# A fused transformer kernel on one core: in the quantised FFN, gated values are quantised two passes behind, the rounding unit comes from a square on ScalarE, and GpSimd has no pass

## The chip, the cores and the metric

The kernel runs on one core of one Trainium2 chip. The metric is the device time of one execution in microseconds (us). Beside it stands one profiled execution, with the start and the duration of every instruction on TensorE (PE; PEld for its weight loads), VectorE (DVE), ScalarE (ACT), GpSimd (POOL) and the DMA queue of SyncE (SP).

## What is computed

Six blocks in a row act on x of 16 x 256 tokens by 128 features: a quantised FFN, an attention of low rank, the quantised FFN again, a mixture of experts, a windowed attention, and the experts again. Only the quantised FFN is touched:

```
def fp4_quant_dequant(x):                       # blocks of 16 along the last axis
    scale = max(max(abs(block)) / 6, 1e-12)
    xn = block / scale
    idx = searchsorted(_MID, abs(xn))           # _MID = .25 .75 1.25 1.75 2.5 3.5 5
    return _GRID[idx] * sign(xn) * scale        # _GRID = 0 .5 1 1.5 2 3 4 6
def fp4_linear(x, w): return quant_dequant(x) @ quant_dequant(w).T
h = silu(fp4_linear(x, w_gate)) * fp4_linear(x, w_up)   # 128 -> 352
x = x + 0.5 * fp4_linear(h, w_down)                     # on layernorm(x)
```

## The kernel before

Everything stays in SBUF as tiles of 128 tokens. An FFN phase (class `Ffn`, run 0 and run 1) makes 16 passes, each over two tiles (256 tokens), and all phases are written engine by engine with semaphores; each engine runs its own list in order. One pass z on each engine:

- ScalarE: normalises the two tiles of pass z+1 into `xh` (L328, one operation a tile), copies the transposed x out of PSUM to `xqT` (L343), copies the transposed h of pass z-2 to `hqT` (L348, L349), and applies silu to the gate product, `sg` (L354).
- VectorE: product of `sg` and the up result in PSUM into the h columns of `xh` (L248, pass z-2), then `quantise` over all 960 columns at once, 256 of x of pass z and 704 of h of pass z-2: block maxima (L101), scale (L104), its inverse (L105, L106), xn = value times inverse (L107), then three operations that make a rounding constant from xn and add it: exponent mask (L114), lower bound (L115), sum (L116). Then the residual add of pass z-3 (L265) and two bn_stats for the next layer norm (L184).
- GpSimd: `dequantise`: subtracts the rounding constant (L140) and multiplies by the scale into `xhq` (L142). L104 of the next pass waits for L142, since it overwrites the scale.
- TensorE: waits for `xhq`; transposes x (L293, 2 matmuls) and h (L299, 6), then gate and up (L307, 8 instructions in the trace), then down (L316, 12).

`rounds` orders the passes: 0 to 2 unrolled, a loop, and three at the end (18 in all). The weights are quantised once at the start by the same two functions, and other phases use `xh`, `xhq`, `q_xn`, `q_mg` for other things. The phases are separated: each engine drains and all wait for each other.

Of the kernel before, what the change touches and what calls it, by code (L numbers as in the profile page):

```python
# [12 lines left out]
F32 = mybir.dt.float32  # L13
# [16 lines left out]
EXPO, HALF = 0x7F800000, 0x00400000  # L30
MAGIC = 1.5 * 2.0 ** 22
NUDGE = 1.0 - 2.0 ** -22

H, DH = 16, 8
SL = 64
# [16 lines left out]
def ds(start, n):  # L52
    return slice(start, start + n) if isinstance(start, int) else bass.ds(start, n)
# [139 lines left out]
class Ffn:  # L193
# [2 lines left out]

    N = NT // 2
    XC, HC_, ALL = (0, 2 * D), (2 * D, 2 * D + 2 * I0), (0, 2 * D + 2 * I0)  # L200

    def __init__(self, k, run):

        self.k, self.run = k, run
        self.x0 = run * self.N
        self.q0 = run * (self.N + 2)
        self.s_xn = k.sem("ffn_xn")
        self.s_xn_read = k.sem("ffn_xn_read")
        self.s_rounded = k.sem("ffn_rounded")
        self.s_minus = k.sem("ffn_minus")  # L210
        self.s_scaled = k.sem("ffn_scaled")
# [10 lines left out]
    def rounds(self, eng, fn, ch=None, per=0):  # L222

        n = self.N
        fn(0, True, False, False)
        fn(1, True, False, False)
        fn(2, True, True, False)
        with eng.Fori(3, n - 1) as z:
            if ch:
                ch.enter(z - 3, per)  # L230
            fn(z, True, True, True)
            if ch:
                ch.leave(n - 4)
        fn(n - 1, True, True, True)
        fn(n, False, True, True)
        fn(n + 1, False, True, True)

    def cols(self, x, h):
        return self.ALL if x and h else self.XC if x else self.HC_

    def vector(self, eng, ch):
        k, v = self.k, self.k.nc.vector
        x0, q0 = self.x0, self.q0

        def fn(z, x, h, back):
            if h:
                eng.wait_ge(self.s_silu, x0 + z - 1)
                v.tensor_tensor(k.xh[:, 2 * D:].rearrange("p (a b) -> p a b", a=2), k.sg[:, :, :],  # L248
                                k.PS[:, 2:4, 0:I0], ALU.mult).then_inc(self.s_h, 1)
                eng.wait_ge(self.s_h, x0 + z - 1)  # L250
            if x:
                eng.wait_ge(self.s_xn, x0 + z + 1)
            free = (self.s_scaled, q0 + z) if not isinstance(z, int) or z or self.run else None
            quantise(k.nc, ch, k.xh, k.qt, self.cols(x, h), free,
                     (self.s_xn_read, x0 + z + 1) if x else None).then_inc(self.s_rounded, 1)
            if back:
                self.add(eng, z - 3)

        self.rounds(eng, fn, ch, QD)
        self.add(eng, self.N - 1)  # L260

    def add(self, eng, i):
        k, v = self.k, self.k.nc.vector
# [5 lines left out]
            bn_stats(k, 2 * i + j)  # L269

    def gpsimd(self, eng, ch):
        k = self.k
        x0, q0 = self.x0, self.q0

        def fn(z, x, h, back):
            eng.wait_ge(self.s_rounded, q0 + z + 1)
            if x and (not isinstance(z, int) or z or self.run):
                eng.wait_ge(self.s_xqT_ps, x0 + z)
            if back or (h and self.run):
                eng.wait_ge(self.s_hqT_ps, x0 + z - 2)  # L280
            dequantise(k.nc, k.xhq, k.qt, self.cols(x, h), (self.s_minus, q0 + z + 1), self.s_scaled)

        self.rounds(eng, fn)

    def tensor(self, eng):
        k, t = self.k, self.k.nc.tensor
        x0, q0 = self.x0, self.q0

        def fn(z, x, h, back):
            eng.wait_ge(self.s_scaled, q0 + z + 1)  # L290
            if x:
                for j in range(2):
                    last = t.transpose(k.PS[:, 4, j * P:(j + 1) * P], k.xhq[:, j * D:(j + 1) * D], k.ident[:, :])  # L293
                last.then_inc(self.s_xqT_ps, 1)
            if h:
                for j in range(2):
                    for c, (o, w) in enumerate(HC):
                        o += 2 * D + j * I0
                        last = t.transpose(k.PS[0:w, 5 + j, c * P:(c + 1) * P], k.xhq[:, o:o + w], k.ident[:, :])  # L299
                last.then_inc(self.s_hqT_ps, 1)  # L300
            if x:
                eng.wait_ge(self.s_xqT, x0 + z + 1)
                if not isinstance(z, int) or z or self.run:
                    eng.wait_ge(self.s_h, x0 + z)
                for j in range(2):
                    for w, bank in ((0, 0), (1, 2)):
                        last = t.matmul(k.PS[:, bank + j, 0:I0], k.xqT[:, j * P:(j + 1) * P], k.wguT[:, w, :],  # L307
                                        start=True, stop=True)
                last.then_inc(self.s_gu_ps, 1)
            if h:  # L310
                eng.wait_ge(self.s_hqT, x0 + z - 1)
                if back:
                    eng.wait_ge(self.s_added, x0 + z - 2)
                for j in range(2):
                    for c, (o, w) in enumerate(HC):
                        last = t.matmul(k.PS[:, 7, j * D:(j + 1) * D], k.hqT[0:w, j, c, :], k.wdT[0:w, c, :],  # L316
                                        start=c == 0, stop=c == 2)
                last.then_inc(self.s_y_ps, 1)

        self.rounds(eng, fn)  # L320

    def scalar(self, eng):
        k, s = self.k, self.k.nc.scalar
        x0, n = self.x0, self.N

        def normalised(i):
            for j in range(2):
                ins = s.activation(k.xh[:, j * D:(j + 1) * D], k.X[:, ds(2 * i + j, 1), :].squeeze(1), ACT.Identity,  # L328
                                   bias=k.nmr[:, ds(2 * i + j, 1)], scale=k.rstd[:, ds(2 * i + j, 1)])
            ins.then_inc(self.s_xn, 1)  # L330

        eng.wait_ge(self.k.sem("statistics_ready"), self.phase + 1)
        normalised(0)

        def fn(z, x, h, back):
            if x:
                if not (isinstance(z, int) and z == n - 1):
                    eng.wait_ge(self.s_xn_read, x0 + z + 1)
                    normalised(z + 1)
                eng.wait_ge(self.s_xqT_ps, x0 + z + 1)  # L340
                if not isinstance(z, int) or z or self.run:
                    eng.wait_ge(self.s_gu_ps, x0 + z)
                s.activation(k.xqT[:, :], k.PS[:, 4, 0:256], ACT.Copy).then_inc(self.s_xqT, 1)  # L343
            if h:
                eng.wait_ge(self.s_hqT_ps, x0 + z - 1)
                if back:
# [3 lines left out]
            if x:  # L350
                eng.wait_ge(self.s_gu_ps, x0 + z + 1)
                if not isinstance(z, int) or z or self.run:
                    eng.wait_ge(self.s_h, x0 + z)
                s.activation(k.sg[:, :, :], k.PS[:, 0:2, 0:I0], ACT.Silu).then_inc(self.s_silu, 1)  # L354

        self.rounds(eng, fn)


class Attention:
# [109 lines left out]
    @staticmethod  # L469
    def later(b, n=1):  # L470

        return not isinstance(b, int) or b >= n
# [686 lines left out]
class Core:  # L1159


    def __init__(self, nc, ctx):
        self.nc, self.ctx, self.sems = nc, ctx, {}

        def sb(name, shape, dt=F32):
            return ctx.enter_context(nc.sbuf_tensor(name, shape, dt))
# [15 lines left out]
        self.xh, self.xhq = (sb(n, [P, 2 * D + 2 * I0]) for n in ("xh", "xhq"))  # L1182
        self.xn, self.xqT = self.xh[:, 0:2 * D].rearrange("p (a b) -> p a b", a=2), sb("xqT", [P, 2 * P])
        self.sg = sb("sg", [P, 2, I0])
        self.hqT = sb("hqT", [P, 2, 3, P])

        self.wa, self.wb = sb("wa", [P, QL + KVL]), sb("wb", [QL + KVL, D + 96])
# [264 lines left out]
```

## Time and profile before

| | us |
|---|---|
| runs of the kernel, median (lowest to highest of 3) | 2058.89 (2056.21 to 2062.37) |
| the profiled execution, own time | 2063.71 |
| its span, first to last instruction | 2061.9 |
| mean TensorE clock granted, share of full | 0.822 |

The profile is read by time first: the first FFN phase lies near the start of the span, the second from about 612 us. A row of the timeline gives start, duration, engine, line of the code, operation, what is written from what, how many are merged, and in square brackets how long the engine had stood idle and what ended that. A granted clock of 1.00 is 2.4 GHz and 0.50 is 1.2 GHz.

### The profile page before, as it was taken

How to read it: one execution, taken by the hardware profiler on the slowest of the kernel's cores; microseconds unless marked ns; L12 is line 12 of the kernel's file. 1: busy time of each engine (PE TensorE's matmuls, PEld its weight loads, DVE VectorE, ACT ScalarE, POOL GpSimd, SP SyncE). 2: the span in 40 equal slices, each digit the busy share in tenths (PEclk: the TensorE clock that was granted, in tenths of full speed). 3: DMA queues.
4: the chain of work that ended last, by engine and by line, in shares of the span. 5: the costliest groups of instructions: out<-in, count | busy, mean ns of one | idle time of the engine just before them, and what ended most of it. 6: DMA issues, size and time to landing. Idle time of an engine off the chain costs nothing.

```text
span 2061.9 us, 34069 instructions
## 1 busy us (share of the span) xinstructions
PE 1301.8 (63%) x10601; PEld 852.2 (41%) x10602; DVE 1045.1 (51%) x2359; ACT 642.5 (31%) x1132; POOL 526.5 (26%) x584
## 2 busy tenths in 40 slices
PE   1566367777756565008999933888887401999891
PEld 0444245445434445005555511555554400555550
DVE  5777455666636773522222255767674442222225
ACT  1222034444443221003333310555555100333330
POOL 1334111111103340472222212212210065222220
PEclk9877578989988875559999975999999555999995
DMA  8500021121200000011111156333231011111114
GB/s 235 66 0 0 16 48 33 36 44 31 38 11 0 0 0 0 30 53 32 34 36 36 35 133 103 55 52 60 45 62 23 0 40 48 35 35 36 35 36 131
DMA packets 194423, 89.80 MB, mean 44 GB/s; under 512 B 128939, under 2 KB 186676, under 8 KB 194356
## 3 DMA queue, kind: packets, MB, share of 16 engines
q1 hardware_dynamic: 185652, 71.02, 17.0%
q0 software_dynamic: 8704, 17.91, 2.4%
q8 instruction: 40, 0.66, 0.1%
q14 instruction: 27, 0.22, 0.0%
HBM read 28.96 MB, written 30.03 MB: 29 GB/s over the span
## 4 chain that ended last, share of the span: by engine, by line
PE 42%; DVE 11%; issue 9%; POOL 9%; DMA 7%; SPq 6%; ACT 1%; DVEq 1%; POOLq 0%; ACTq 0%
PE PS L913 13%; PE PS L939 7%; POOL slots L1127 5%; DMA qT<-qs 5%; SPq L811 4%; PE PS L580 3%; PE PS L929 3%; PE PS L501 2%; PE PS L549 2%; PE PS L307 2%; PE PS L565 2%; SPq L1282 1%; POOL ks L767 1%; PE PS L537 1%; PE PS L878 1%
## 5 line engine op out<-in xcount | busy, mean ns | idle before, releaser
L913 PE MATMUL PS<-wgu,xTs 128*128 x584 | 306.3, 608 | 25.7 <-issue 24.6
L639 ACT ACTIVATE pt<-PS 128x768 f32<-128x768 f32 (+1 forms) x256 | 234.2, 918 | 257.5 <-PE PS L501 256.2
L1020 DVE TENSOR_TENSOR pt<-pt,PS 128x512 f32<-128x512 f32 x146 | 100.5, 688 | 338.6 <-PE PS L913 305.6
L1132 POOL DMA_INDIRECT outs<-ys,xs x144 | 137.9, 957 | 418.3 <-DVE ys L1028 412.1
L720 DVE TENSOR_REDUCE m<-PS 128x4 f32<-128x1024 f32 x128 | 156.2, 1224 | 95.2 <-PE PS L501 93.9
L720 DVE TENSOR_REDUCE sg<-PS 128x6 f32<-128x768 f32 x128 | 122.1, 955 | 128.8 <-PE PS L501 127.5
L501 PE MATMUL PS<-tables 64*128 64x192 bf16 (+2 forms) x2048 | 184.6, 260 | 0.0
L965 ACT ACTIVATE pt<-PS 128x512 f32<-128x512 f32 x146 | 87.2, 597 | 294.7 <-PE PS L913 294.7
L939 PE MATMUL PS<-wdn,pt 128*128 x1152 | 163.5, 285 | 21.4 <-issue 19.6
L1127 POOL DMA_INDIRECT slots<-xr,ix x128 | 122.8, 960 | 209.8 <-DVE ix L1011 188.5
L939 PEld LDWEIGHTS PS<-wdn,pt 128*128 128x128 f32 x1152 | 139.4, 191 | 79.7 <-issue 79.6
L905 PE MATMUL PS<-ident,xs 128*128 128x128 f32 x148 | 41.2, 279 | 193.5 <-DMA xs<-slots 193.4
L140 POOL TENSOR_TENSOR q_mg<-q_xn,q_mg 128x960 f32<-128x960 f32 (+3 forms) x37 | 74.1, 2004 | 284.3 <-DVE q_xn L116 284.3
L960 ACT ACTIVATE xTs<-PS 128x128 f32<-128x128 f32 x148 | 41.1, 278 | 254.2 <-PE PS L905 254.2
L905 PEld LDWEIGHTS PS<-ident,xs 128*128 128x128 f32 x148 | 21.0, 142 | 237.1 <-issue 218.6
L307 PE MATMUL PS<-wguT,xqT 128*128 128x352 f32 x256 | 113.3, 602 | 4.3 <-ACT xqT L343 4.3
L549 PE MATMUL PS<-kT,qT 64*128 64x128 bf16 (+1 forms) x704 | 69.8, 280 | 72.8 <-DMA qT<-qs 68.6
L501 PEld LDWEIGHTS PS<-tables 64*128 64x128 bf16 x2048 | 104.9, 102 | 12.1
L913 PEld LDWEIGHTS PS<-wgu,xTs 128*128 128x128 f32 x584 | 90.1, 194 | 36.7 <-issue 36.7
L580 PE MATMUL PS<-pt,v 128*32 128x256 f32 (+1 forms) x1408 | 99.9, 400 | 6.7 <-ACT pt L639 5.9
L929 PEld LDWEIGHTS PS<-ident,pt 128*128 128x128 f32 x576 | 72.4, 142 | 76.7 <-issue 75.3
L293 PE MATMUL PS<-ident,xhq 128*128 128x128 f32 x64 | 17.6, 367 | 129.6 <-POOL xhq L142 129.6
(196 smaller groups left out, 2298.5 us busy)
## 6 DMA issues: line engine op xcount, KB each, us to landing
slots<-empty SPq DMA_DIRECT2D x38, 258.0 KB, 9.9
xs<-slots SPq DMA_DIRECT2D x152, 64.5 KB, 1.8
pt<-outs SPq DMA_DIRECT2D x16, 512.0 KB, 4.2
outs<-ys,xs POOLq DMA_INDIRECT x144, 2.2
wgu<-in_L_ffn_w_gate SPq DMA_DIRECT2D x1, 2048.0 KB
wgu<-in_L_ffn_w_up SPq DMA_DIRECT2D x1, 2048.0 KB
wdn<-in_L_ffn_w_down SPq DMA_DIRECT2D x8, 256.0 KB
qT<-hqT SPq DMA_DIRECT2D x128, 4.0 KB
```

Source lines behind the costliest of these rows:

```text
L307: last = t.matmul(k.PS[:, bank + j, 0:I0], k.xqT[:, j * P:(j + 1) * P], k.wguT[:, w, :], start=True, stop=True)
L501: last = t.matmul(cols(k.PS[:, self.bank + u, :]), k.eye2[rows, e, :], table[rows], start=False, stop=e == 1, skip_group_check=True)
L549: t.matmul(k.PS[:, self.bank + u, c:c + n], k.qT[p][rows, a, j * P:(j + 1) * P], k.kT[p][rows, kg, 0:n], start=j == 0, stop=False, skip_gr ...
L580: last = t.matmul(k.PS[32 * u:32 * u + 32, 0, col:col + n], k.v[p][:, kb, g, :], k.pt[:, (2 * a + u // 2) % 4, u % 2, c:c + n], start=kb = ...
L639: s.activation(k.pt[:, a % 4, :, 0:w], k.PS[:, self.bank:self.bank + 2, 0:w], ACT.Exp, scale=self.scale).then_inc(self.s_p, 1)
L720: v.tensor_reduce(out, src, AX.X, ALU.max).then_inc(self.s_nat_read, 1)
L913: t.matmul(k.PS[:, 1 + 2 * p + w, :], k.xTs[:, p, :], k.wgu[:, w, ds(e, 1), :].squeeze(1), start=True, stop=True).then_inc((self.s_gate_ps ...
L929: last = t.transpose(k.PS[:, 5, c * P:(c + 1) * P], k.hs[:, p, c * P:(c + 1) * P], k.ident[:, :])
L939: last = t.matmul(k.PS[:, 6, 0:D], k.hTs[:, p, c * P:(c + 1) * P], k.wdn[:, ds(e, 1), c, :].squeeze(1), start=c == 0, stop=c == FC - 1)
L1020: v.tensor_tensor(k.hs[:, p, :], k.sgs[:, p, :], k.PS[:, 2 + 2 * p, :], ALU.mult).then_inc(self.s_h, 1)
L1127: g.indirect_dma_start(k.slots, bass.IndirectOffsetOnAxis(ap=k.ix[:, u, r:r + 1], axis=0), k.xr[:, u, r, :], None).then_inc(self.s_sc[u], 16)
L1132: g.indirect_dma_start(k.outs, bass.IndirectOffsetOnAxis(ap=k.xs[:, u, D:D + 1].bitcast(I32), axis=0), k.ys[:, u, :], None).then_inc(self. ...
```

## The change

GpSimd's part of an FFN pass goes: subtraction and scaling are done on VectorE. The rounding constant is no longer made by L114 and L115; ScalarE squares xn with a factor, writing `mg` (L382 of the new kernel), and VectorE adds it in one operation (L290) and subtracts it in another (L291), both with the constant `BASE`. The scaling is split in x (256 columns) and h (704), each with a semaphore of its own, `ffn_xq` and `ffn_hq` (L298). `xh`, `q_xn` and `q_mg` get a second buffer each in the space of the attention's `qT` tiles, and the scales a tile `fscale` with two halves. Normalising runs two passes ahead. The product for the gated values of pass z-1 now stands in pass z after xn, and they are quantised in pass z+1, so that their transposes come two passes behind their x. There are 21 steps instead of 18 and the loop is unrolled by two.

```diff
+BINADE, BASE = 2.0 ** 23 / 12, 2.0 ** 23 * 2 / 3
+    STEPS, FIRST = N + 5, 4
...
+        def quantised(z, p):
...
+            ch.run(v.tensor_reduce(amax, blocks, AX.X, ALU.max, apply_absolute_value=True))
+            if x and self.later(z, 2):
+                eng.wait_ge(self.s_xq, x0 + z - 1)
+            if self.has(z - 4) or (h and self.run):
+                eng.wait_ge(self.s_hq, x0 + z - 3)
+            ch.run(v.tensor_scalar(scale, amax, -1.0 / 6.0, -1e-12, ALU.mult, ALU.min))
+            ch.run(v.reciprocal(inv, scale))
+            ch.run(v.tensor_scalar(inv, inv, -NUDGE, None, ALU.mult))
+            last = v.tensor_tensor(xn.rearrange("p (n k) -> p n k", k=BLK), blocks,
+                                   inv.unsqueeze(2).broadcast_to([P, n, BLK]), ALU.mult)
+            last.then_inc(self.s_xn_read, 1)
...
+        def fn(z, p):
+            if self.has(z) or self.has(z - 2):
+                quantised(z, p)
+            if self.has(z - 1):
+                eng.wait_ge(self.s_silu, x0 + z)
...
+            if self.has(z - 4):
+                self.add(eng, z - 4)
+            if self.has(z) or self.has(z - 2):
+                eng.wait_ge(self.s_sq, q0 + z + 1)
...
+                ch.run(v.scalar_tensor_tensor(xn, mg, BASE, xn, ALU.add, ALU.add))
+                ch.run(v.scalar_tensor_tensor(mg, mg, BASE, xn, ALU.add, ALU.subtract))
...
     def gpsimd(self, eng, ch):
...
+        pass
...
+                eng.wait_ge(self.s_xn_read, q0 + z + 1)
...
+                s.activation(k.fmg[p][:, c], k.fxn[p][:, c], ACT.Square, scale=BINADE ** 0.5).then_inc(self.s_sq, 1)
...
+            squared(z + 1, 1 - p)
+            if self.has(z):
+                eng.wait_ge(self.s_gu_ps, x0 + z + 1)
...
+        again = [x[:, :, :].rearrange("p g t -> p (g t)").bitcast(F32) for x in self.qT]
+        self.fxh, self.fxn, self.fmg = [self.xh, again[0]], [self.qt["xn"], again[1]], [self.qt["mg"], again[2]]
```

VectorE, one pass of the loop, before (`xh` holds the values, `sg` the silu, `q_xn` and `q_mg` the two rounding operands):

```order
L248 TENSOR_TENSOR xh<-sg,PS 128x704 [waits ffn_silu]
...
L101 TENSOR_REDUCE q_amax<-xh 128x60 [waits ffn_xn]
...
L104 TENSOR_SCALAR q_scale<-q_amax 128x60 [waits ffn_scaled,vector_chain]
...
L107 TENSOR_TENSOR q_xn<-xh,q_inv 128x960 [waits vector_chain]
L114 TENSOR_SCALAR q_mg<-q_xn 128x960 [waits ffn_xn_read]
...
L115 TENSOR_SCALAR q_mg<-q_mg 128x960 [waits vector_chain]
...
L116 SCALAR_TENSOR_TENSOR q_xn<-q_xn,q_mg 128x960 [waits vector_chain]
...
L265 SCALAR_TENSOR_TENSOR X<-PS,X 128x256
```

And the same after:

```order
L265 TENSOR_REDUCE q_amax<-xh 128x60 [waits ffn_h]
...
L270 TENSOR_SCALAR fscale<-q_amax 128x60 [waits ffn_hq]
...
L273 TENSOR_TENSOR q_xn<-xh,q_inv 128x960 [waits vector_chain]
...
L282 TENSOR_TENSOR qT<-sg,PS 128x704 [waits ffn_silu]
...
L308 SCALAR_TENSOR_TENSOR X<-PS,X 128x256
...
L290 SCALAR_TENSOR_TENSOR q_xn<-q_mg,q_xn 128x960 [waits ffn_squares]
...
L291 SCALAR_TENSOR_TENSOR q_mg<-q_mg,q_xn 128x960 [waits vector_chain]
...
L298 TENSOR_TENSOR xhq<-q_mg,fscale 128x256 [waits ffn_xqT_ps,vector_chain]
...
L298 TENSOR_TENSOR xhq<-q_mg,fscale 128x704 [waits ffn_hqT_ps]
```

The product moved from the head of a pass to behind xn, two single-input operations went, and a second rounding operation and two scalings came.

ScalarE, the tail of one pass of the loop, before:

```order
L343 ACTIVATE xqT<-PS 128x256
L345 REGISTER_ALU
L347 REGISTER_ALU
L348 ACTIVATE hqT<-PS 128x2x256
L349 ACTIVATE hqT<-PS 96x2x128
L354 ACTIVATE sg<-PS 128x704
```

And after (the second of the two unrolled passes, `q_mg` is the square):

```order
L366 ACTIVATE qT<-X,nmr,rstd 128x128
L382 ACTIVATE q_mg<-q_xn 128x960
L399 ACTIVATE sg<-PS 128x704
L404 ACTIVATE hqT<-PS 128x2x256
L405 ACTIVATE hqT<-PS 96x2x128
```

The square, which belongs to the next pass, stands directly ahead of silu, and silu moved ahead of the copies of h; no table load stands between.

TensorE, one pass of the loop, before:

```order
L293 MATMUL PS<-ident,xhq 128x128 x2
L299 MATMUL PS<-ident,xhq 128x128 x2
L299 MATMUL PS<-ident,xhq 96x128
...
L307 MATMUL PS<-wguT,xqT 128x352 x4
L316 MATMUL PS<-wdT,hqT 128x128 x6
```

And after:

```order
L328 MATMUL PS<-ident,xhq 128x128 x2
L336 MATMUL PS<-wdT,hqT 128x128 x6
L345 MATMUL PS<-wguT,xqT 128x352 x4
L355 MATMUL PS<-ident,xhq 128x128 x2
L355 MATMUL PS<-ident,xhq 96x128
```

The down matmuls moved from the end to right behind the x transposes, and the h transposes to the end.

## Rows read from the trace of the kernel before

**Rows 1.** Both FFN phases: stretch, its length, busy time (count) by engine, clock, DMA

```profile
38.70:211.80 173.10, 103.64 (x448) 76.99 (x448) 122.19 (x209) 46.06 (x97) 65.27 (x36) 0.80 0.23 33
612.40:788.50 176.10, 105.07 (x448) 77.38 (x448) 122.11 (x209) 46.13 (x97) 65.29 (x36) 0.77 0.00 0
```

**Rows 2.** Waits, first phase: who, for whom, us in total, times, longest

```profile
POOL q_mg L140 <- DVE q_xn L116: 106.7, 18, 10.6
PE PS L293 <- POOL xhq L142: 63.7, 15, 9.9
...
DVE X L265 <- PE PS L316: 26.5, 10, 6.2
```

**Rows 3.** Timeline of TensorE, first phase: start, duration, instruction

```profile
62.06 0.69 PE L293 MATMUL PS<-ident,xhq 128*128 128x128 f32 x2 [7.43 <-POOL xhq L142]
...
72.15 2.62 PE L307 MATMUL PS<-wguT,xqT 128*128 128x352 f32 x8
...
142.74 0.69 PE L293 MATMUL PS<-ident,xhq 128*128 128x128 f32 x2 [6.30 <-POOL xhq L142]
...
144.50 3.01 PE L307 MATMUL PS<-wguT,xqT 128*128 128x352 f32 x8
...
189.77 0.44 PE L293 MATMUL PS<-ident,xhq 128*128 128x128 f32 x2 [1.47 <-POOL xhq L142]
```

**Rows 4.** Timeline of the other engines, one pass and a half of the loop

```profile
67.05 2.22 POOL L140 TENSOR_TENSOR q_mg<-q_xn,q_mg 128x960 f32<-128x960 f32 x1 [5.04 <-DVE q_xn L116]
...
67.95 0.76 ACT L354 ACTIVATE sg<-PS 128x704 f32<-128x704 f32 x1 [3.01 <-PE PS L307]
...
69.34 1.82 POOL L142 TENSOR_TENSOR xhq<-q_mg,q_scale 128x960 f32<-128x960 f32 x1
...
71.64 1.15 DVE L101 TENSOR_REDUCE q_amax<-xh 128x60 f32<-128x960 f32 x1
...
75.04 0.66 DVE L114 TENSOR_SCALAR q_mg<-q_xn 128x960 int32<-128x960 int32 x1
...
76.43 1.16 DVE L116 SCALAR_TENSOR_TENSOR q_xn<-q_xn,q_mg 128x960 f32<-128x960 f32 x1
77.50 0.42 DVE L265 SCALAR_TENSOR_TENSOR X<-PS,X 128x256 f32 x1
...
78.07 0.53 DVE L184 BATCH_NORM_STATS2 bn<-X  x2
78.69 0.89 DVE L248 TENSOR_TENSOR xh<-sg,PS 128x704 f32<-128x704 f32 x1
```

**Rows 5.** Busy time by stretch; the granted clock stands third from the end

```profile
81.90:87.60 5.70, 5.69 (x15) 0.51 0.00 0
87.60:93.00 5.40, 3.75 (x26) 1.00 0.00 0
...
148.80:151.80 3.00, 0.05 (x1) 0.00 (x0) 2.43 (x5) 0.27 (x1) 2.92 (x2) 1.00 0.00 0
...
175.90:180.60 4.70, 0.00 (x0) 0.00 (x0) 3.29 (x6) 0.20 (x1) 3.98 (x2) 0.89 0.00 0
180.70:186.50 5.80, 5.79 (x15) 4.11 (x16) 4.55 (x7) 1.25 (x3) 0.90 (x1) 0.51 0.00 0
```

**Rows 6.** Single prices: timeline, groups by line, and one line's smallest, median, largest (ns)

```profile
45.13 1.28 ACT L354 ACT_TABLE_LOAD   x1
...
45.16 4.96 PE L307 MATMUL PS<-wguT,xqT 128*128 128x352 f32 x8 [0.47 <-ACT xqT L343]
...
200.63 2.93 PE L316 MATMUL PS<-wdT,hqT 128*128 128x128 f32 x12 [0.95 <-ACT hqT L349]
...
L639 ACT ACTIVATE pt<-PS x256: 804/917/1032, 273.0 to 1594.9; 128x768 f32<-128x768 f32 x64, 128x1024 f32<-128x1024 f32 x64
...
L960 ACT ACTIVATE xTs<-PS 128x128 f32<-128x128 f32 x148 | 41.1, 278 | 254.2 <-PE PS L905 254.2
...
L328 ACT ACTIVATE xh<-X,nmr,rstd 128x128 f32 x24 | 10.4, 484 | 0.4 <-DVE q_xn L107 0.2 <-issue 0.2
```

More of the change, by code:

```diff
@@ L199 @@
     N = NT // 2
-    XC, HC_, ALL = (0, 2 * D), (2 * D, 2 * D + 2 * I0), (0, 2 * D + 2 * I0)
+    STEPS, FIRST = N + 5, 4
+    HID = 2 * D
     def __init__(self, k, run):
@@ L208, in __init__ @@
         self.s_xn_read = k.sem("ffn_xn_read")
+        self.s_sq = k.sem("ffn_squares")
         self.s_rounded = k.sem("ffn_rounded")
-        self.s_minus = k.sem("ffn_minus")
-        self.s_scaled = k.sem("ffn_scaled")
+        self.s_xq = k.sem("ffn_xq")
+        self.s_hq = k.sem("ffn_hq")
         self.s_xqT_ps = k.sem("ffn_xqT_ps")
@@ L220, in __init__, with has, later, walk @@
         self.s_added = k.sem("ffn_added")
[L222 to L228, printed above, removed]
+    def has(self, i):
+        return not isinstance(i, int) or 0 <= i < self.N
+    def later(self, i, n=1):
+        return self.run or not isinstance(i, int) or i >= n
+    def walk(self, eng, fn, ch=None, per=0):
+        for z in range(self.FIRST):
+            fn(z, z % 2)
+        passes = (self.N - 2 - self.FIRST) // 2
+        with eng.Fori(0, passes) as m:
@@ L229, in rounds @@
             if ch:
-                ch.enter(z - 3, per)
-            fn(z, True, True, True)
+                ch.enter(m, 2 * per)
+            for i in range(2):
+                fn(2 * m + (self.FIRST + i), i)
             if ch:
[L233 to L239, printed above, removed]
+                ch.leave(passes)
@@ L241, in vector @@
+        for z in range(self.FIRST + 2 * passes, self.STEPS):
+            fn(z, z % 2)
     def vector(self, eng, ch):
         k, v = self.k, self.k.nc.vector
[L243 to L250, printed above, removed]
+        x0, q0, HID = self.x0, self.q0, self.HID
@@ L251, in fn @@
+        def quantised(z, p):
+            x, h = self.has(z), self.has(z - 2)
+            c = slice(0 if x else HID, k.FW if h else HID)
+            b = slice(c.start // BLK, c.stop // BLK)
+            n = b.stop - b.start
+            src, xn, mg, scale = k.fxh[p][:, c], k.fxn[p][:, c], k.fmg[p][:, c], k.fscale[:, p, b]
+            blocks = src.rearrange("p (n k) -> p n k", k=BLK)
+            amax, inv = k.qt["amax"][:, b], k.qt["inv"][:, b]
             if x:
                 eng.wait_ge(self.s_xn, x0 + z + 1)
-            free = (self.s_scaled, q0 + z) if not isinstance(z, int) or z or self.run else None
@@ L254, in fn @@
[L254 to L260, printed above, removed]
+            if h:
+                eng.wait_ge(self.s_h, x0 + z - 1)
+            ch.run(v.tensor_reduce(amax, blocks, AX.X, ALU.max, apply_absolute_value=True))
+            if x and self.later(z, 2):
+                eng.wait_ge(self.s_xq, x0 + z - 1)
@@ L262, in add @@
+        self.walk(eng, fn, ch, 6)
     def add(self, eng, i):
@@ L271, in gpsimd, with fn @@
     def gpsimd(self, eng, ch):
[L272 to L283, printed above, removed]
+        pass
     def tensor(self, eng):
         k, t = self.k, self.k.nc.tensor
-        x0, q0 = self.x0, self.q0
-        def fn(z, x, h, back):
-            eng.wait_ge(self.s_scaled, q0 + z + 1)
+        x0, HID = self.x0, self.HID
+        def fn(z, p):
+            x, h, down = self.has(z), self.has(z - 2), self.has(z - 3)
             if x:
+                eng.wait_ge(self.s_xq, x0 + z + 1)
+                if self.later(z):
+                    eng.wait_ge(self.s_xqT, x0 + z)
                 for j in range(2):
@@ L294, in fn @@
                 last.then_inc(self.s_xqT_ps, 1)
-            if h:
+            if down:
+                eng.wait_ge(self.s_hqT, x0 + z - 2)
+                if self.later(z - 3):
+                    eng.wait_ge(self.s_added, x0 + z - 3)
                 for j in range(2):
                     for c, (o, w) in enumerate(HC):
-                        o += 2 * D + j * I0
-                        last = t.transpose(k.PS[0:w, 5 + j, c * P:(c + 1) * P], k.xhq[:, o:o + w], k.ident[:, :])
-                last.then_inc(self.s_hqT_ps, 1)
+                        last = t.matmul(k.PS[:, 7, j * D:(j + 1) * D], k.hqT[0:w, j, c, :], k.wdT[0:w, c, :],
+                                        start=c == 0, stop=c == 2)
+                last.then_inc(self.s_y_ps, 1)
             if x:
                 eng.wait_ge(self.s_xqT, x0 + z + 1)
-                if not isinstance(z, int) or z or self.run:
+                if self.later(z):
                     eng.wait_ge(self.s_h, x0 + z)
@@ L310, in fn, with normalised @@
             if h:
-                eng.wait_ge(self.s_hqT, x0 + z - 1)
-                if back:
-                    eng.wait_ge(self.s_added, x0 + z - 2)
+                eng.wait_ge(self.s_hq, x0 + z - 1)
+                if self.later(z - 2):
+                    eng.wait_ge(self.s_hqT, x0 + z - 2)
                 for j in range(2):
                     for c, (o, w) in enumerate(HC):
[L316 to L320, printed above, removed]
+                        o += HID + j * I0
+                        last = t.transpose(k.PS[0:w, 5 + j, c * P:(c + 1) * P], k.xhq[:, o:o + w], k.ident[:, :])
+                last.then_inc(self.s_hqT_ps, 1)
+        self.walk(eng, fn)
     def scalar(self, eng):
         k, s = self.k, self.k.nc.scalar
-        x0, n = self.x0, self.N
-        def normalised(i):
+        x0, q0, HID = self.x0, self.q0, self.HID
+        def normalised(i, p):
             for j in range(2):
-                ins = s.activation(k.xh[:, j * D:(j + 1) * D], k.X[:, ds(2 * i + j, 1), :].squeeze(1), ACT.Identity,
+                ins = s.activation(k.fxh[p][:, j * D:(j + 1) * D], k.X[:, ds(2 * i + j, 1), :].squeeze(1), ACT.Identity,
                                    bias=k.nmr[:, ds(2 * i + j, 1)], scale=k.rstd[:, ds(2 * i + j, 1)])
@@ L349, in fn @@
                 s.activation(k.hqT[0:96, :, 2, :], k.PS[0:96, 5:7, 256:384], ACT.Copy).then_inc(self.s_hqT, 1)
[L350 to L356, printed above, removed]
+        self.walk(eng, fn)
 class Attention:
@@ L1184, in __init__ @@
         self.sg = sb("sg", [P, 2, I0])
+        self.FW = 2 * D + 2 * I0
+        self.fscale = sb("fscale", [P, 2, self.FW // BLK])
         self.hqT = sb("hqT", [P, 2, 3, P])
```

44 lines of the change are left out of this document (35 added, 9 removed).

## The prediction

> **What bounds the kernel now.** Only the two quantised FFN phases are touched, so I read first how long they last: from the first normalised tile to the last statistics 172.9 us (38.8 to 211.7) and 176.0 us (612.5 to 788.5), which the rows of busy time by stretch frame [rows 1]. No engine is full there: VectorE is busy 122 of 173 us, TensorE 104, GpSimd 65, ScalarE 46. So a ring of waits sets the pace, and the waits say which: TensorE's first transposes of a pass wait for GpSimd's xhq, GpSimd for VectorE's last rounding step, and VectorE's residual add for TensorE [rows 2]. TensorE's blocks give the period: their first transposes start at 62.06 and, 13 passes later, at 189.77 us, 9.82 us a pass [rows 3]. The ring is VectorE's scale to rounding (71.64 to 77.59 less the reduce of 1.15 that stands ahead, 4.8 us) and then 2.22 and 1.82 us on GpSimd [rows 4], some 9.1 us with the hand-overs when nothing else is late.
>
> Next, TensorE's clock. A block of matmuls starts low (0.51, that is the 1.2 GHz level) after the engine has stood still for 4.7 us, and stays low for 5.7 us of uninterrupted work in the block at 81.9, after which the next row shows 1.00 (2.4 GHz) [rows 5]. In the block at 142.74 its gate and up matmuls take 3.01 us; the usual high-clock figure is 2.62, in the block at 72.15. The 0.39 us more is 0.78 us at the low clock, so there the rise came about 2.6 us into the block [rows 3]. That is the shortest low stretch I find at a low start. In before this hardly matters: TensorE's results are used late, and only the add waits for them.
>
> **The change part by part.** *GpSimd leaves the ring.* Gone from every pass are the subtraction and the scaling, 2.22 and 1.82 us [rows 4], a hand-over before each, and with them the wait of L104. This alone would be 4.2 us a pass of the ring.
>
> *VectorE's work.* Removed: two single-input passes of 0.66 us (L114, L115). Kept: one rounding pass of 1.16. Added: a second of 1.16 (the subtraction) and the two scalings. No scaling stands on VectorE today; its two-tensor operations take 0.42 for 256 elements (L265) and 0.89 for 704 (the product L248), and I take those [rows 4]. VectorE gains 1.16+0.42+0.89-1.32 = 1.15 us a pass.
>
> Its new chain, read from the starts in the timeline [rows 4]: (a) from the product for the gated values to the end of the x scaling, product 0.80 (0.89, less the 0.09 by which L265 starts before L116 ends), add 0.57, statistics 0.62, two rounding passes of 1.19 each, x scaling 0.42: 4.8 us. (b) From the end of the x scaling, h scaling 0.8, then reduce to the end of xn 3.37 (71.64 to 75.01): 4.2 us. If nothing else were late, 4.8+4.2 = 9.0 us, below today's 9.82.
>
> *What now comes late.* The product waits for silu, and two things hold silu. First ScalarE's own order: the square of pass z+1 stands ahead of silu of pass z, and it waits for xn of z+1. A 960-element square has no row. Silu takes 0.76 for 704 elements [rows 4], the exponentials up to 1.03 for 1024, so 0.97 from PSUM; a 128-element operation takes 0.48 from SBUF and 0.28 from PSUM [rows 6], so up to 1.17 from SBUF. I take 1.08, between the two. Silu then ends at 4.2+0.04+1.08+0.66 = 6.0 us after the x scaling at the earliest. The wait on the square itself, ahead of the rounding, is covered: product, add and statistics (2.0 us) stand between. Queued behind the product on VectorE are the add, the rounding and both scalings, on which TensorE's next block waits.
>
> Second TensorE: in the new order its block is x transposes, the 12 down matmuls, then gate and up, then h transposes. Before, gate and up came ahead of down; now down stands ahead of them. At the high clock gate and up end 0.3+1.35+2.6 = 4.25 us after the block starts, ahead of the square. At the low clock the 12 down matmuls take 2.9 (200.63), and the 8 gate and up 4.96 (45.16) [rows 6]. With the clock low for t us, and t above 3.3, they end at G = t + 2.45(1-(t-3.3)/4.8) + 0.15: for t = 5.7, 7.1 us; for the short case of 2.6 us, about 5.5 us.
>
> Does the block start low? A block has some 5.0 us of work high and 7.4 mixed; in a pass of 10.7 to 12.5 us about 5 us of standing still are left. In before, after 3.0 us without a matmul (148.8 to 151.8) the block still began at the high clock, and after 4.7 us (175.9 to 180.6) at the low [rows 5]. Five is on the low side, so I take every block as starting low.
>
> The period is then G plus hand-over and silu and hand-over (0.05+0.05+0.76+0.05) plus chain (a) 4.8, so G + 5.7: 11.2 us for the short case, 12.8 for the long one. The rows have both, and I take the middle, 12.0. Silu's bound by the square, 6.0, is met in both (5.5+0.1+0.8 is 6.4).
>
> *Start and end of a phase.* x of pass 0 is ready 4.4 us in (narrow operations, 0.42 us for 256 elements); passes 1 to 3 have no down matmuls and partly narrow operations, by the same chain 8.7, 9.7 and 9.9 us; passes 4 to 15 are 12 at 12.0 = 144. The drain is one step longer than before: one pass without x (12.4), one with h alone (6.2), and then transposes, copies, down, add and statistics at the low clock (1.5+0.9+2.9+0.4+0.6 and the hand-overs, 7.2), 25.8 us. Sum 202.5 us.
>
> *Everything else* (attention, the experts, quantising the weights) keeps its instructions. The new buffers lie in the space of three attention tiles that are idle in these phases. I cost them at nothing; a phase starts only when all engines have ended the one before.
>
> **The sum.** First phase 202.5-172.9 = +29.6, second 202.5-176.0 = +26.5, together +56. The profiled execution took 2063.7 us beside its span of 2061.9, so it would become 2120; it lay 4.8 above the median of the runs. Against that median, 2058.9+56 = 2115 us. The change goes from a GpSimd-VectorE ring of 9.8 us to one through TensorE at its low clock of 12.0.
>
> **Rivals.** (1) *The clock stays high.* Then silu is bound by the square: 6.0+0.05+4.8 = 10.8 us a pass, with start and drain 178.4 us a phase, +5.5 and +2.4: 2067 us. For it: a block that follows 3 us of rest begins high. Against: the rest here is about 5. Chance 0.10, split evenly at the bound of 0.3% (6.2 us, about what a measurement of this kernel can tell from no change).
>
> A rule of the Trainium skill speaks for something near it: "TensorE: Matmul & The Clock Gate", What's actually happening, says that for modelling the ramp penalty is below 1% of a typical kernel's span. By that at most 20 us would come on top of 2067, up to 2087. The trace does not agree, since in this phase the 1.2 GHz stretches come back pass after pass; I leave it 0.04.
>
> (2) *Faster.* It is one mechanism. The place is ScalarE's queue between square and silu. If the clock stays high and the square is done by the time gate and up end, the period is 4.25+5.7 = 9.95, and a phase 167 us: -6 and -9, 2044 us. It decides from the point where xn plus square end earlier than 4.3 us after the x scaling; my rows put them at 5.3. Chance 0.08.
>
> (3) *The clock falls only before every other block*, as it did before. The mean period is 11.4, 24 passes by 0.6 less: 2100 us. For it: that is the pattern of the trace. Against: there the rests were unequal (1.5 and 6 us), and the new ring has equal ones. Chance 0.14.
>
> (4) *The clock never rises inside a block.* G is 0.5+2.8+5.0 = 8.2, the period 13.9, +1.9 by 24: 2161 us. For it: the last passes of before, which have less work, stay low. Against: blocks with more work do rise. Chance 0.09.
>
> A table load for each switch between square and silu is another thought. "ScalarE: Activation LUTs", Table sets, of the Trainium skill says that functions of different sets cost a load at each switch, and square is not among those it lists as shared. By it two loads of 1.28 us a pass [rows 6] would give a period of 13.5 and 2150 us; but the built order has no load between them, so it gets no chance of its own.
>
> **Numbers.** Forecast 2115 with chance 0.55; its own bounds, 0.8 us by 24 passes, are 2096 to 2134. The range takes in (1) and (3) and leaves out (2) and (4): 2065 to 2140. Faster by over 0.3%: 0.08, from (2); within: 0.05, half of (1); slower: 0.87, the rest.
>
> **What would show it.** In the new profile VectorE's product should be the group with the large idle time, released by silu, some 2.5 us a pass; silu by the gate and up matmuls and not by the square; TensorE's period near 12 us, its blocks beginning at 0.5. If the product waits for silu while silu waits for VectorE's xn, rival (1) or (2) holds. The forecast is wrong if TensorE's blocks begin at 1.0, or if the rests between them are under 3 us.

## The result, and the profile after

| | before | after |
|---|---|---|
| median of 4 runs (lowest to highest), us | 2058.49 (2056.21 to 2062.37) | 2119.56 (2116.81 to 2121.51) |
| profiled execution, own time / span | 2063.71 / 2061.9 | 2118.19 / 2116.4 |
| mean granted clock of TensorE | 0.822 | 0.817 |
| first and second FFN phase, us | 172.9 and 176.0 | 199.6 and 201.8 |

The changed kernel takes 1.0283 of the time before, with a 95% interval of 1.0262 to 1.0304: 61 us slower by the medians, 54.5 by the two spans. The two phases account for 26.7 + 25.8 = 52.5 us of the span's 54.5. The 6.6 us between the two differences is the place of the profiled executions: that of before lay 5.2 above its median, that of after 1.4 below.

Busy time by stretch of after, the phases first, then four stretches of the loop (columns as in [rows 1] and [rows 5]: length, busy time and count of PE, PEld, DVE, ACT, POOL, then the granted clock):

```profile
38.58:238.19 199.61, 116.62 (x448) 88.22 (x448) 135.53 (x222) 60.50 (x115) 0.00 (x0) 0.78 0.20 29
643.98:845.77 201.79, 118.95 (x448) 89.01 (x448) 135.54 (x222) 60.77 (x115) 0.00 (x0) 0.75 0.00 0
95.35:101.30 5.95, 5.95 (x20) 4.84 (x21) 3.88 (x6) 2.15 (x4) 0.00 (x0) 0.52 0.01 3
...
107.80:112.00 4.20, 4.20 (x18) 3.81 (x19) 3.80 (x6) 1.29 (x4) 0.00 (x0) 0.59 0.00 0
119.10:125.00 5.90, 5.90 (x20) 4.69 (x21) 3.84 (x6) 2.15 (x4) 0.00 (x0) 0.51 0.00 0
126.70:131.50 4.80, 0.00 (x0) 0.00 (x0) 4.42 (x8) 0.89 (x3) 0.00 (x0) 1.00 0.00 0
```

GpSimd is empty. VectorE went from 122 to 136 us of busy time, and still stands idle for a third of the phase. TensorE is busy 117 us where it was 104 [rows 1], for the same 448 instructions: more of them run at the low clock. The stretches show it: about the first 4 to 6 us of work of each block at 0.51 to 0.59, after 4.8 us with no matmul at all.

Waits in the first phase (who, for whom, us in total, times, longest):

```profile
PE PS L328 <- DVE xhq L298: 78.6, 16, 9.1
...
DVE qT L282 <- ACT sg L399: 27.7, 8, 3.8
DVE xh L282 <- ACT sg L399: 23.9, 8, 5.7
...
ACT sg L399 <- PE PS L345: 21.1, 16, 2.8
```

These answer to [rows 2]. The hand-overs between VectorE and GpSimd are gone. In their place stands a ring over three engines: VectorE's product (L282) waits for silu, silu for the gate and up matmuls (L345), and TensorE's block (L328) for VectorE's scaling. The product waits 51.6 us in 16 passes, 3.2 us a pass.

TensorE in two passes of the loop (start, duration, instruction; L328 x transposes, L336 down, L345 gate and up, L355 h transposes), the rows that answer to [rows 3]:

```profile
107.80 0.67 PE L328 MATMUL PS<-ident,xhq 128*128 128x128 f32 x2 [4.92 <-DVE xhq L298]
108.26 2.77 PE L336 MATMUL PS<-wdT,hqT 128*128 128x128 f32 x12
110.82 2.75 PE L345 MATMUL PS<-wguT,xqT 128*128 128x352 f32 x8
113.41 0.82 PE L355 MATMUL PS<-ident,xhq 128*128 128x128 f32 x6
119.06 0.69 PE L328 MATMUL PS<-ident,xhq 128*128 128x128 f32 x2 [4.84 <-DVE xhq L298]
...
119.54 2.76 PE L336 MATMUL PS<-wdT,hqT 128*128 128x128 f32 x12
122.10 3.92 PE L345 MATMUL PS<-wguT,xqT 128*128 128x352 f32 x8
```

The 12 down matmuls take 2.77 us in both blocks, their low-clock time; gate and up take 2.75 (all but high) in the one and 3.92 in the other. From the block's start to their end it is 5.8 and 7.0 us. The blocks alternate so through the loop: 84.25 and 179.33 are starts eight passes apart, 95.08 us, 11.89 a pass.

VectorE and ScalarE in the same place, one pass, to be laid beside [rows 4]:

```profile
107.24 1.23 DVE L298 TENSOR_TENSOR xhq<-q_mg,fscale 128x256 f32<-128x256 f32 x2
...
110.58 1.16 DVE L273 TENSOR_TENSOR qT<-qT,q_inv 128x960 f32<-128x960 f32 x1
...
111.86 1.00 ACT L382 ACTIVATE qT<-qT 128x960 f32<-128x960 f32 x1 [2.13 <-DVE qT L273]
...
113.61 0.76 ACT L399 ACTIVATE sg<-PS 128x704 f32<-128x704 f32 x1 [0.75 <-PE PS L345]
...
114.40 0.89 DVE L282 TENSOR_TENSOR xh<-sg,PS 128x704 f32<-128x704 f32 x1 [2.66 <-ACT sg L399]
...
116.22 1.14 DVE L290 SCALAR_TENSOR_TENSOR qT<-qT 128x960 f32<-128x960 f32 x1
...
117.39 1.16 DVE L291 SCALAR_TENSOR_TENSOR qT<-qT 128x960 f32<-128x960 f32 x1
...
118.58 1.23 DVE L298 TENSOR_TENSOR xhq<-qT,fscale 128x256 f32<-128x256 f32 x2
```

xn is ready at 111.74 and the square at 112.86, but silu starts at 113.61, when gate and up end, and the product at 114.40. Had silu followed the square at once, the product would have started 0.7 us earlier in this pass; in the next one, where gate and up end at 126.0 and the square at 124.2, 1.8 us.

### The profile page after: what moved, and what is told of

Its sections match the earlier page's. It is cut to its first block, busy times and chain, and to the rows that moved or that the text cites. A ratio compares the mean times of both kernels' runs of the same rounds, so it can differ in the third digit from the quotient of the medians.

```text
span 2116.4 us, 33913 instructions
## 1 busy us (share of the span) xinstructions
PE 1329.1 (63%) x10601; PEld 875.1 (41%) x10602; DVE 1071.3 (51%) x2387; ACT 671.5 (32%) x1168; POOL 396.6 (19%) x512
## 4 chain that ended last, share of the span: by engine, by line
PE 36%; DVE 9%; issue 8%; POOL 5%; DMA 5%; SPq 3%; ACT 1%; DVEq 1%; ACTq 0%; POOLq 0%
PE PS L964 12%; PE PS L990 7%; POOL slots L1178 5%; PE PS L980 3%; PE PS L345 3%; DMA qT<-qs 3%; PE PS L336 2%; PE PS L631 2%; SPq L862 1%; SPq L1337 1%; PE PS L929 1%; PE PS L552 1%; PE PS L600 1%; PE PS L588 1%; DVE X L1092 1%
## 5 line engine op out<-in xcount | busy, mean ns | idle before, releaser
L964 PE MATMUL PS<-wgu,xTs 128*128 x584 | 305.2, 606 | 25.8 <-issue 24.8
L328 PE MATMUL PS<-ident,xhq 128*128 128x128 f32 x64 | 20.1, 413 | 157.7 <-DVE xhq L298 157.7
L345 PE MATMUL PS<-wguT,xqT 128*128 128x352 f32 x256 | 115.3, 609 | 2.8 <-ACT xqT L390 2.8
L336 PE MATMUL PS<-wdT,hqT 128*128 128x128 f32 (+1 forms) x384 | 86.6, 413 | 10.3 <-ACT hqT L405 7.2
```

The costliest lines, as they stand in the source:

```text
L964: t.matmul(k.PS[:, 1 + 2 * p + w, :], k.xTs[:, p, :], k.wgu[:, w, ds(e, 1), :].squeeze(1), start=True, stop=True).then_inc((self.s_gate_ps ...
```

## The experiments

**Theory A** is the prediction's: the ring runs through TensorE, and its low clock is what makes it 12 us long; the down matmuls lie ahead of gate and up at that clock. **Rival B:** silu is held in ScalarE's queue by the square, which waits for VectorE. **Theory D** in the expectations: the low clock is only a symptom, and VectorE or ScalarE sets the pace. A third thought is that only VectorE's added work was lost. "Unused" matmuls below multiply the identity by itself into a free part of PSUM: they add work and leave nothing out. Ratios are to the kernel before, run on the same chip beside each; the experiments ran on three chips, so they are best compared with each other by ratio.

### TensorE's order: gate and up ahead of down

```diff
-            if down:
-                eng.wait_ge(self.s_hqT, x0 + z - 2)
...
-                last.then_inc(self.s_y_ps, 1)
...
                 last.then_inc(self.s_gu_ps, 1)
+            if down:
+                eng.wait_ge(self.s_hqT, x0 + z - 2)
...
+                last.then_inc(self.s_y_ps, 1)
             if h:
```

> The changed kernel with TensorE's order of the pass as before: gate and up right behind the x transposes, the down matmuls behind them. Theory A (silu is held by gate and up, which end late because the 12 down matmuls of 2.8 us at the low clock stand ahead of them): gate and up then end about 6.0 us after the block starts with a long low stretch and 4.8 with a short one, where silu meets the bound of the square (6.0). The period falls from 11.9 to about 11.3, 24 passes by 0.6: 2120 - 15 = 2105 us. Theory B (silu is held by the square that stands ahead of it on ScalarE): no change, 2120.

Measured: 2087.03 us (2082.37 to 2097.58), ratio 1.0155 (1.0117 to 1.0192), phases 185.4 and 187.5. The gain is 26 us by the ratios and 32 by the medians, about twice the 15 that A gave, and B, by which nothing should change, falls as the sole cause. In this experiment (L336 is now gate and up, L345 down):

```profile
137.47 0.44 PE L328 MATMUL PS<-ident,xhq 128*128 128x128 f32 x2 [3.50 <-DVE xhq L298]
138.38 4.13 PE L336 MATMUL PS<-wguT,xqT 128*128 128x352 f32 x8 [0.47 <-ACT xqT L390]
142.34 1.50 PE L345 MATMUL PS<-wdT,hqT 128*128 128x128 f32 x12
```

A shorter ring also shortens TensorE's rest, from 4.9 to 3.5 us, and now most blocks begin at the high clock (0.44 for the transposes instead of 0.69). But the clock still falls within the block: gate and up take 4.13 us, not 2.62. The square (from 141.61, 1.00 us) ended here 0.1 us after gate and up, so it would be what holds silu if TensorE were any quicker.

### ScalarE's order: silu ahead of the next pass's square

```diff
-            squared(z + 1, 1 - p)
             if self.has(z):
                 eng.wait_ge(self.s_gu_ps, x0 + z + 1)
...
+            squared(z + 1, 1 - p)
```

> The changed kernel with silu of pass z ahead of the square of pass z+1 on ScalarE. Theory A (gate and up hold silu): between -2 and 0 us, 2118 to 2120, since silu starts when gate and up end in both. Theory B (the square holds silu): about 1 us less in each of 24 to 30 passes, 2090 to 2096 us. Theory C (the added work on VectorE is the bound): no change either, but then the product's idle time would not be there.

Measured: 2114.20 us (2110.83 to 2118.64), ratio 1.0264 (1.0241 to 1.0288), phases 200.6 and 200.1. That is 4 to 6 us below what A gave and some 20 above B, with an interval that overlaps that of the changed kernel; the two phases together are 0.7 us shorter than in the changed kernel. B falls as the cause: with the square out of the way, silu waits the longer for TensorE, 54.6 us in the passes from 60 to 200 us where the changed kernel has 15.1, and the product waits as before, 38.2 us against 37.5. The waits in that stretch:

```profile
ACT sg L398 <- PE PS L345: 54.6, 12, 5.2
...
DVE qT L282 <- ACT sg L398: 22.1, 6, 3.8
DVE xh L282 <- ACT sg L398: 16.1, 6, 2.8
```

With both orders changed at once:

> The changed kernel with both orders turned (gate and up ahead of down, silu ahead of the square) and no unused matmuls. Theory A: TensorE's blocks still begin low after 3.5 us of rest or fall soon behind their start, so gate and up take 4.1 to 5.1 us as with the first order alone, and silu gains 0.1 us in every other pass: 2083 to 2087 us. Theory B (the square's place was worth a share of its own once gate and up are early): 2065 to 2075.

Measured: 2091.82 us (2083.62 to 2093.68), ratio 1.0145 (1.0110 to 1.0180), phases 186.3 and 186.9. That is within the noise of gate and up first alone, and 5 us above A's range. While the clock falls in the block, silu's place in ScalarE's queue is worth nothing.

### The clock held up by unused matmuls, in the changed kernel

The first try put 30 of them behind the h transposes of every pass:

```diff
                 last.then_inc(self.s_hqT_ps, 1)
+            for j in range(30):
+                t.matmul(k.PS[:, 4, 256:384], k.ident[:, :], k.ident[:, :], start=True, stop=True)
```

> The changed kernel with 30 matmuls of 128 columns, which compute nothing that is used, at the end of each TensorE pass, in the 4.9 us in which the engine stands still. They cost about 3.6 us at the high clock and leave 2 us of rest. Theory A (the low clock at the start of each block makes the pass 11.9 us): blocks begin at 1.00, gate and up end 4.3 us after the start, the square becomes the bound, the period falls to 10.7: 24 passes by 1.2, and some at start and drain: 2120 - 30 to 35 = 2085 to 2090 us. Theory D (the clock is a symptom, VectorE or ScalarE sets the pace): 2120 or later.

Measured: 2160.77 us (2157.21 to 2164.17), ratio 1.0500 (1.0473 to 1.0528). A miss of the experiment's design, not of A: I had taken the price of half a matmul.

```profile
126.21 6.86 PE L358 MATMUL PS<-ident 128*128 128x128 f32 x60
...
241.90 20.26 PE L358 MATMUL PS<-ident 128*128 128x128 f32 x180
```

Each float32 matmul is two instructions of 0.114 us, so 30 of them last 6.86 us where the rest was 4.9. In the loop TensorE never stood still between passes, each pass took 11.28 us because its own work did, and some 20 us ran on behind each phase's last tile. The next two fit the rest, stand only in passes with x and h, and have 16 and 20 of them:

```diff
                 last.then_inc(self.s_hqT_ps, 1)
+                for j in range(16 if x else 0):
+                    t.matmul(k.PS[:, 4, 256:384], k.ident[:, :], k.ident[:, :], start=True, stop=True)
```

> The changed kernel with 16 unused matmuls (32 instructions of 0.114 us at the high clock, 3.7 us) at the end of a TensorE pass, only in passes that have both x and h. It mends the run with 30, in which they took 6.9 us a pass, more than the rest they were to fill, and 20 us ran on behind the last tile of each phase. Theory A (low clock): period 10.5 us (xn ends 4.1 us after the x scaling, square 1.0, silu 0.7, product to x scaling 4.6), the phases 180 us instead of 199.6 and 201.8: 2119.6 - 41 = 2079 us. Theory D (the clock is a symptom): 2115 or later.

> The changed kernel with 20 unused matmuls (40 instructions, 4.6 us), which leave 0.9 us of rest in a pass of 10.5 us. With 16 the rest was 2.0 to 2.2 us and the clock fell in 4 of 12 passes. Theory A: no low stretch once it is high, every pass 10.45 us: some 5 us a phase below the run with 16, 2086 - 10 = 2076 us.

Measured with 16: 2085.59 us (2081.45 to 2087.88), ratio 1.0116 (1.0088 to 1.0144); with 20: 2076.23 us (2073.78 to 2079.15), ratio 1.0078 (1.0059 to 1.0098), phases 179.0 and 180.7. With 16 the rest was mostly 2.0 to 2.2 us, and the clock still fell in 4 of the first phase's 12 loop passes, as in this one:

```profile
104.92 0.43 PE L328 MATMUL PS<-ident,xhq 128*128 128x128 f32 x2 [2.20 <-DVE xhq L298]
105.20 1.72 PE L336 MATMUL PS<-wdT,hqT 128*128 128x128 f32 x12
106.71 4.08 PE L345 MATMUL PS<-wguT,xqT 128*128 128x352 f32 x8
```

With 20 the rest was 0.9 to 1.3 us and it never fell inside the loop:

```profile
124.47 0.43 PE L328 MATMUL PS<-ident,xhq 128*128 128x128 f32 x2 [1.30 <-DVE xhq L298]
124.74 1.54 PE L336 MATMUL PS<-wdT,hqT 128*128 128x128 f32 x12
126.12 2.53 PE L345 MATMUL PS<-wguT,xqT 128*128 128x352 f32 x8
```

Gate and up now end 4.2 us after the block's start, and the pass is 10.4 to 10.6 us. So the low clock costs the changed kernel some 43 us (42 by the ratios), 2% of its time. This is not its share of the loss, for the kernel before gains 21 us in the same way (below): with the clock held up in both, the changed kernel is still slower by 37 of the 58 us that it lost by ratio (1.0078 against 0.9900). Now rival B's mechanism is the one that binds. ScalarE in the same pass:

```profile
128.53 1.01 ACT L384 ACTIVATE qT<-qT 128x960 f32<-128x960 f32 x1 [2.37 <-DVE qT L273]
129.44 0.74 ACT L401 ACTIVATE sg<-PS 128x704 f32<-128x704 f32 x1
```

Silu starts the moment the square is through, 0.8 us after gate and up have ended at 128.65.

### Orders and clock together

The edits above combined: 14 unused matmuls and silu ahead of the square, with down still first, as shown; then 8, and 12, with gate and up first as well:

```diff
+                for j in range(14 if x else 0):
+                    t.matmul(k.PS[:, 4, 256:384], k.ident[:, :], k.ident[:, :], start=True, stop=True)
...
-            squared(z + 1, 1 - p)
...
+            squared(z + 1, 1 - p)
```

> The changed kernel with silu ahead of the square and 14 unused matmuls (3.2 us); the down matmuls stay ahead of gate and up. Theory A: once the clock is high the square is what holds silu (passes of 10.4 us in the run with 16); without it gate and up do, 4.1 us after the block starts, and a pass is 9.6 us: 24 passes by 0.85 below the run with 16, 2086 - 20 = 2066 us. If the square never counts: 2086.

> The changed kernel with gate and up ahead of the down matmuls, silu ahead of the square, and 8 unused matmuls (1.8 us) in such passes. Theory A: all three things that hold silu are gone, it ends 4.2 us after the x scaling as xn does, and VectorE alone sets a period of 8.9 us: phases of 153 to 158 us, 2058 - 35 = 2015 to 2025 us, the fastest. If one of the three still holds silu, 9.5 us or more a pass and 2040 or later.

> Both orders turned as before, with 12 unused matmuls (24 instructions, 2.75 us) instead of 8. With 8 the clock still fell in two passes of three: 10.8 us with the low stretch and 9.12 without it (124.50 to 133.62), where the rest was 1.75 us. With 12 the rest is some 0.9 us. Theory A: every pass 9.12 us, bound by VectorE's own chain; 12 passes by 1.1 us less in each phase: 2070 - 26 = 2044 us, which is not below the kernel before with such matmuls (2037): the change's best pace then equals the old ring's 9.15 and its longer start and drain are lost. If something beside the clock holds the passes of 10.8 us: 2070.

| unused, order | us (lowest to highest) | ratio (95%) | phases |
|---|---|---|---|
| 14, silu first | 2061.92 (2052.59 to 2066.00) | 1.0002 (0.9987 to 1.0018) | 173.4, 172.3 |
| 8, both | 2070.27 (2064.75 to 2076.64) | 1.0050 (1.0032 to 1.0068) | 178.7, 177.5 |
| 12, both | 2048.74 (2044.73 to 2054.20) | 0.9940 (0.9918 to 0.9961) | 166.4, 166.4 |

The first came near its expectation: silu's place, worth nothing before, is worth 0.8 us a pass and 16 us in all once the clock stays up. The second missed by some 50 us. With 8 unused matmuls and rests of 1.7 to 1.8 us the clock fell in two passes of three; but that is under half of the miss (22 us by the ratios to the run with 12). The rest is the expectation's own: it took passes of 8.9 us and phases of 153 to 158, and with the clock up they are 9.11 and 166.4. The third came 5 us above its expectation, with every loop pass but the first and the last two at 9.11 us. One of its passes (L336 gate and up), and the busy time of eight:

```profile
111.22 0.44 PE L328 MATMUL PS<-ident,xhq 128*128 128x128 f32 x2 [0.82 <-DVE xhq L298]
...
112.13 2.63 PE L336 MATMUL PS<-wguT,xqT 128*128 128x352 f32 x8 [0.47 <-ACT xqT L392]
...
114.80 0.76 ACT L400 ACTIVATE sg<-PS 128x704 f32<-128x704 f32 x1 [1.96 <-PE PS L336]
...
115.59 0.89 DVE L282 TENSOR_TENSOR qT<-sg,PS 128x704 f32<-128x704 f32 x1 [0.26 <-ACT sg L400]
```

```profile
92.99:165.90 72.91, 61.96 (x417) 51.81 (x417) 66.66 (x105) 29.28 (x56) 0.00 (x0) 1.00 0.00 0
```

VectorE is busy 66.7 of 72.9 us, and idle ahead of the product for 0.26 us in this pass and 3.0 us in all eight. This is the pace of the new division of work with the waits all but gone: VectorE's own.

### The clock held up in the kernel before

```diff
                 last.then_inc(self.s_y_ps, 1)
+            for j in range(14):
+                t.matmul(k.PS[:, 4, 256:384], k.ident[:, :], k.ident[:, :], start=True, stop=True)
```

> The kernel before with 14 such matmuls at the end of each TensorE pass (1.7 us at the high clock). Theory A: in before the low clock costs too, in every other pass (10.7 to 11.3 us instead of 9.15), since the residual add waits for the down matmuls; the period falls from 9.9 to 9.15, 26 passes by 0.75: 2058 - 20 = 2038 us. If the clock played no part before, as the prediction's sentence on it says (it hardly matters there), 2055 to 2058.

The second one has them only in passes with x and h:

> The kernel before with 14 unused matmuls only in passes that have both x and h, so that none stands behind the last tile. Theory A: as with them in every pass (2037), less some 3 us at the end of each phase: 2030 to 2034 us.

Measured: 2037.19 us (2031.90 to 2039.91), ratio 0.9900 (0.9877 to 0.9922), phases 161.6 twice; and 2037.28 us (2035.14 to 2046.23), ratio 0.9901 (0.9866 to 0.9936), phases 164.6 and 165.4. The first is as expected, although its expectation prices 14 unused matmuls at 1.7 us, half of the 3.3 that the trace has (the same slip as with the 30). The second missed its 2030 to 2034: with none of them outside the full passes, the last down matmuls of a phase ran at the low clock (2.93 us instead of 1.60), the drain took 2.0 us more, and the stretch ahead of it 1.1 us more in the first phase and 1.8 in the second. Eight passes of the first:

```profile
89.88:163.10 73.22, 64.08 (x449) 55.23 (x449) 60.38 (x96) 22.17 (x48) 32.40 (x16) 1.00 0.00 0
```

That is 9.15 us a pass where before had 9.82 on average in the first phase [rows 3]. These two kernels are the quickest of the study, and faster than both the one before and the one after.

## Why the prediction was right, and where it was not

The forecast was 2115 us, the time is 2119.56: inside the range, on the forecast's side, and by its mechanism. Of its steps:

- **Start, loop, drain.** The x transposes of the first pass start 4.47 us into the phase, those of the next three 9.21, 9.73 and 10.12 us apart, against 4.4, 8.7, 9.7 and 9.9; the twelve passes of the loop take 142.0 us against 144; the drain 24.1 against 25.8. Phases 199.6 and 201.8 against 202.5 twice: the sum of +56 was 3.5 too high for +52.5. The median rose more than the profiled span only because the profiled execution of before lay high.
- **VectorE's chains.** From the product to the x transposes 4.6 us (114.40 to 119.06), against 4.8 to the end of the x scaling; from those transposes to the end of xn some 4.0, against 4.2. Both scalings were priced right by operations of the same kind: 1.23 for the two together, against 0.42 + 0.8.
- **The square.** It took 1.00 us, where the bounds were 0.97 and 1.17 and I took 1.08. By the page "ScalarE: Activation LUTs", Table sets, of the Trainium skill each switch of set costs a load; here it costs nothing, since in the loop no load stands between square and silu in the trace, as the prediction took from the built order.
- **The clock.** After 4.7 to 4.9 us of rest the blocks of the loop, all but one, begin low or fall before their down matmuls; "about 5" was right. G was bounded by 5.5 and 7.1 and measured 5.8 and 7.0. I took the middle between a short and a long case without knowing which would come; they came in turn, 11.3 and 12.5 us, whose mean is the 11.9. That the middle fits to 0.1 us is luck; nothing in the working gave it.
- **Rival 1, clock stays high.** Its price was good: 10.8 us a pass, and with 20 unused matmuls it is 10.4 to 10.6; its phase of 178.4 us, given without working, became 179.0 and 180.7. Its condition was not. I had set it at rests under 3 us, by a block of before that began high after 3.0 us [rows 5]. That a block begins high does not mean that it stays so, and the trace of before had this already: the very block that begins high after 3.0 us falls in its first microsecond (granted clock 0.62 from 152.00 to 153.20), and its gate and up take 3.73 us instead of 2.62. With gate and up first and rests of 3.3 to 3.6 us the clock was low for a part of every loop block, with 2.0 to 2.2 of some. The block of before:

```profile
151.88 0.44 PE L293 MATMUL PS<-ident,xhq 128*128 128x128 f32 x2 [3.03 <-POOL xhq L142]
...
153.30 3.73 PE L307 MATMUL PS<-wguT,xqT 128*128 128x352 f32 x8
```

- **Rival 2.** 9.95 us a pass was to come if the square came early enough; with silu ahead of it and the clock high it is 9.7. The forecast's place for the next wait, ScalarE's queue, was the right one, and it was hidden for the reason given.
- **Rivals 3 and 4.** Neither came. In the loop every block has its low stretch and not every other one, and in every block the clock rises again before the h transposes (0.82 us each).
- **The rule on the ramp.** "TensorE: Matmul & The Clock Gate", What's actually happening, of the Trainium skill puts the ramp penalty below 1% of a typical kernel's span. These two kernels, in which the low stretch comes back pass after pass, do not agree: holding the clock up gives 43 us of 2120 here, 2.0%, and 21 us of 2058, 1.0%, in the kernel before.
- **The step that failed** is a sentence ahead of the sum: that in before the low clock "hardly matters", since TensorE's results are used late. Two phases of 161.6 instead of 172.9 and 176.0 us say otherwise, 1% of the time. The prediction had the difference in its own numbers, a ring of 9.1 us best and 9.82 on average, and did not ask where the 0.7 came from. The second phase of before shows it more plainly, with starts 9.1 and 11.3 us apart in turn. It did no harm to the sum, which starts from the measured phases, but it hid the cheaper improvement.

The rows of after that bear on the drain, TensorE at the end of the first phase:

```profile
202.98 0.44 PE L328 MATMUL PS<-ident,xhq 128*128 128x128 f32 x2 [4.67 <-DVE xhq L298]
203.25 2.62 PE L336 MATMUL PS<-wdT,hqT 128*128 128x128 f32 x12
...
221.84 1.58 PE L336 MATMUL PS<-wdT,hqT 128*128 128x128 f32 x12 [1.54 <-DVE X L308]
...
234.28 2.93 PE L336 MATMUL PS<-wdT,hqT 128*128 128x128 f32 x12 [0.95 <-ACT hqT L405]
```

The drain was 1.7 us shorter than the forecast, with its first down matmuls (221.84) still at the high clock; the two groups behind them, at 229.12 and 234.28, took 2.93, as priced. The block at 202.98 begins high, but its down matmuls take 2.62 us, so the clock falls at once.

Where the 58 us by ratio went: the low clock costs the changed kernel 42 (1.0283 to 1.0078), but the kernel before 21 (to 0.9900), so some 21 of the 58 are the clock's (16 of 52.5 by the lengths of the phases). The other 37 are there with the clock up in both. Of these, silu ahead of the square takes off 16 (to 1.0002), gate and up ahead of down 13 (to 0.9940), and 8 are left. The clock's part is shown with one edit in each kernel; the two orders' parts have other counts of unused matmuls as well and are taken in this sequence, so they are rough. In what is left a pass of the loop takes 9.11 us against 9.15 for the old ring at the same clock: taking GpSimd out bought almost nothing, since the work that it did now fills VectorE. The phases are 166.4 us against 161.6, so the difference lies in the longer start and drain. VectorE's added work is thus the limit behind the others, and not the cause of the loss.

What stays open is which of the unused matmuls are needed: no count but 14 was tried in the kernel before, nor was any way of keeping TensorE active with work of the kernel's own.

## What to carry to other kernels

Before an engine is taken out of a ring, write down the ring that will close next, and price its TensorE part at the low clock wherever rests of some microseconds stand between short blocks. In such a place try a few unused matmuls in the rest, sized by their traced duration, on the kernel as it is before rebuilding its schedule: two lines gave 1.0% here, where the new schedule at its best, with unused matmuls too, gave 0.6%.

## What the runs showed of the hardware that I had not expected

- The clock falls after rests far shorter than the 4.7 us that I read from before. In the loops with 12 and 20 unused matmuls, with rests of 0.7 to 1.3 us, it stayed at 1.00. With rests of 1.7 to 1.8 us it fell in two passes of three in the kernel with 8, and in one of 24 in the kernel with 14; with 2.0 to 2.2 in some passes.
- How long one rest is does not decide it by itself. In the kernel before, none of the 12 loop blocks that follow a rest of 1.4 to 2.0 us falls (gate and up 2.60 to 2.63 us). In the kernel with 12 unused matmuls, the block at 73.19, behind a rest of only 1.25 us and a block that had run low after 4.58 us of rest, falls: its gate and up take 4.07 us.
- The fall can come inside a block, 1 us and more after it began at 2.4 GHz (gate and up first: block at 137.47, gate and up from 138.38, 4.13 us for what takes 2.62).
- Matmuls that compute nothing are worth their time: 14 a pass, 3.3 us, make the kernel before 21 us faster.
- A float32 matmul of 128 columns is two instructions of 0.114 us each at the high clock.
